# An RWKV block on eight cores: PSUM copies moved from VectorE to ScalarE, one product moved from VectorE to GpSimd

## The reference, cut to what matters

```python
xn = layer_norm(x, ln1_w, ln1_b);  lx = time_shift(xn)            # x: [8, 4096, 1024] f32
k = (xn*time_mix_k + lx*(1-time_mix_k)) @ w_key                   # v, r likewise
sr = sigmoid(r);  w = exp(time_decay)
# per channel, over t (numerically stabilised in the reference):
#   out_t = (A_t + e^(u+k_t) v_t) / (B_t + e^(u+k_t))
#   A_(t+1) = e^(-w) A_t + e^(k_t) v_t ;  B_(t+1) = e^(-w) B_t + e^(k_t)
x1 = x + (out*sr) @ w_output
xn2 = layer_norm(x1, ...);  fk, fr = projections of its time mixes
y = layer_norm(x + x1 + sigmoid(fr) * (square(relu(fk)) @ f_w_value))
out = layer_norm(y + (silu(y@Wg.T) * (y@Wu.T)) @ Wd.T)            # Wg, Wu, Wd from int32, scale 1/127
```

## Time and profile before

| | us |
|---|---|
| median of 3 timed runs | 5509.81 |
| lowest and highest of them | 5486.03, 5567.28 |
| the profiled execution | 5275.61 |
| its span, slowest core (core 3) | 5274.0 |
| shortest span of a core | 5226.8 |
| VectorE busy | 1458.3 (28%) |
| ScalarE busy | 881.8 (17%) |
| GpSimd busy | 145.7 (3%) |
| TensorE matmul busy | 2883.7 (55%) |

### The profile page before, as it was taken

One profiled execution on the slowest core, in us unless ns is written; L12 is line 12 of the kernel. 1 busy time (PEld: TensorE's weight loads), 2 busy tenths in 40 slices (PEclk: granted clock), 3 DMA queues, 4 the chain that ended last, 5 costly groups with the idle time before them and its releaser, 6 DMA issues.

```text
span 5274.0 us, 42491 instructions; the slowest of 8 cores (5226.8 to 5274.0 us)
## 1 busy us (share of the span) xinstructions
PE 2883.7 (55%) x14080; PEld 1449.4 (27%) x14080; DVE 1458.3 (28%) x2032; ACT 881.8 (17%) x1222; POOL 145.7 (3%) x328
## 2 busy tenths in 40 slices
PE   0444444520001777777773576765399999164554
PEld 0211121210000544444442232332144444021222
DVE  2233333236771444443441111111011111010101
ACT  1011111003221222223221112111011111001111
POOL 1100000000000000000000000000000000000000
PEclk9977767765555888888887787887699999587777
DMA  5333333443317222212215524332411010413132
GB/s 104 92 103 96 96 92 84 122 153 129 149 64 147 72 69 80 80 61 81 79 39 118 153 80 136 104 104 74 86 34 62 33 64 25 112 56 112 56 112 72
DMA packets 351012, 472.56 MB, mean 90 GB/s; under 512 B 83536, under 2 KB 263760, under 8 KB 345680
## 3 DMA queue, kind: packets, MB, share of 16 engines
q1 hardware_dynamic: 111488, 218.11, 12.7%
q10 hardware_dynamic: 215552, 186.67, 10.9%
q0 software_dynamic: 23760, 65.07, 6.9%
HBM read 293.65 MB, written 203.42 MB: 94 GB/s over the span
## 4 chain that ended last, share of the span: by engine, by line
issue 26%; PEld 19%; DMA 18%; DVE 12%; DVEq 8%; ACT 7%; ACTq 4%; PEldq 4%; another core or an unknown queue 2%; POOLq 1%; POOL 0%; SPq 0%
PEld psum L340 17%; DVEq L106 7%; DMA v_fm<-arena 4%; ACTq L106 4%; DMA k_fm<-arena 3%; PEldq L106 3%; DMA r_fm<-arena 3%; DMA arena<-h_fm 2%; DMA arena<-wd_bf 2%; ACT arena L297 2%; PEld psum L350 1%; POOLq L106 1%; DVE arena L498 1%; DVE arena L494 1%
## 5 line engine op out<-in xcount | busy, mean ns | idle before, releaser
L340 PE MATMUL psum<-arena 128*128 128x512 bf16 (+1 forms) x13312 | 2691.5, 364 | 1672.4 <-DMA arena<-wo 526.7
L340 PEld LDWEIGHTS psum<-arena 128*128 128x128 bf16 x13312 | 1334.3, 102 | 3024.9 <-issue 1998.8
L350 PE MATMUL psum<-arena 128*128 128x128 f32 x768 | 192.1, 380 | 689.0 <-ACTq L106 640.9
L297 ACT ACTIVATE arena<-arena 128x1024 f32<-128x1024 f32 x128 | 133.6, 1045 | 2327.8 <-DVEq L106 1496.0
L350 PEld LDWEIGHTS psum<-arena 128*128 128x128 f32 x768 | 115.1, 189 | 770.3 <-issue 770.3
L778 DVE SCALAR_TENSOR_TENSOR arena<-psum,arena 128x512 bf16<-128x512 f32 x192 | 123.7, 686 | 729.2 <-ACTq L106 729.2
L574 DVE TENSOR_SCALAR arena<-psum 128x256 f32<-128x256 f32 x512 | 181.6, 417 | 381.3 <-PEq L106 233.1
L392 DVE COPY arena<-psum 128x512 f32<-128x512 f32 x192 | 119.3, 684 | 434.3 <-DMA v_fm<-arena 163.2
L821 DVE SCALAR_TENSOR_TENSOR arena<-psum,arena 128x512 f32<-128x512 f32 x64 | 44.3, 692 | 672.5 <-PEq L106 663.1
L705 DVE SCALAR_TENSOR_TENSOR arena<-psum,arena 128x512 f32<-128x512 f32 x64 | 44.3, 692 | 670.9 <-PEq L106 664.9
L772 ACT ACTIVATE arena<-psum 128x512 bf16<-128x512 f32 x192 | 104.2, 594 | 610.6 <-PEq L106 604.2
(11 more groups left out here) (75 smaller groups left out, 879.6 us busy)
## 6 DMA issues: line engine op xcount, KB each, us to landing
fk_fm<-arena ACTq DMA_DIRECT2D x16, 2048.0 KB, 8.8
arena<-fk_fm SPq DMA_DIRECT2D x8, 4096.0 KB, 30.3
h_fm<-arena ACTq DMA_DIRECT2D x8, 3072.0 KB, 11.7
arena<-h_fm SPq DMA_DIRECT2D x8, 3072.0 KB, 16.9
arena<-x SPq DMA_DIRECT2D x8, 2048.0 KB, 9.2
k_fm<-arena ACTq DMA_DIRECT2D x64, 256.0 KB, 2.7
v_fm<-arena ACTq DMA_DIRECT2D x64, 256.0 KB, 2.7
r_fm<-arena ACTq DMA_DIRECT2D x64, 256.0 KB, 2.2
```

The costliest lines, as they stand in the source:

```text
L297: e.activation(dump.ap[:, q, :], xa[:, q, :], AF.Square, accum_out=stat.ap[:, 4 + q:5 + q])
L340: last = e.matmul(psumb.ap[:, 0:n], lts[i], rhs[i], start=(i == 0), stop=(i == cnt - 1))
L350: last = e.transpose(bank.ap[:, idx * 128:(idx + 1) * 128], ap, ident.ap)
```

## The change

Three things are done. (1) In stage 1 the four copies of `evac4` become ScalarE activations with the function Copy, in ScalarE's queue. (2) In stage 2 the product `ekv` goes to GpSimd as a tensor_tensor. `ek` gets two buffers and `rb` one instead of two. (3) In stage 2 the two scans are emitted as one operation, with one wait ahead and one drain behind them, and so are the first two combinations.

```diff
--- before.py
+++ after.py
@@ -389,9 +389,9 @@
 
                 def evac4(e, jobs=jobs, sgs=sgs):
                     for k4 in range(4):
-                        e.tensor_copy(sgs[k4].ap, jobs[k4][0].ap)
+                        e.activation(sgs[k4].ap, jobs[k4][0].ap, AF.Copy)
                     return e.nop()
-                B.op("vector", evac4, reads=[j[0] for j in jobs], writes=sgs)
+                B.op("scalar", evac4, reads=[j[0] for j in jobs], writes=sgs)
                 for k4, oc in enumerate(range(ob, ob + 4)):
                     B.op("scalar", lambda e, dst=dst, oc=oc, t0=t0, sg_=sgs[k4]: e.dma_start(
                         dst[oc * 128:(oc + 1) * 128, t0:t0 + 512], sg_.ap),
@@ -450,8 +450,8 @@
     ar.mark()
     kb2 = [ar.f32([128, 4096], f"kb{j}") for j in range(2)]
     vb2 = [ar.f32([128, 4096], f"vb{j}") for j in range(2)]
-    rb2 = [ar.f32([128, 4096], f"rb{j}") for j in range(2)]
-    ek = ar.f32([128, 4096], "ek")
+    rb = ar.f32([128, 4096], "rb")
+    ek2 = [ar.f32([128, 4096], f"ek{j}") for j in range(2)]
     ekv = ar.f32([128, 4096], "ekv")
     tmp = ar.f32([128, 4096], "tmp")
     Abuf = ar.f32([128, 4100], "Abuf")
@@ -465,7 +465,7 @@
 
     if debug_phases >= 2:
         for j in range(DC):
-            kb, vb, rb = kb2[j % 2], vb2[j % 2], rb2[j % 2]
+            kb, vb, ek = kb2[j % 2], vb2[j % 2], ek2[j % 2]
             yb, kmax = yb2[j % 2], kmax2[j % 2]
             for src, hb, b in ((k_fm, HB["k_fm"], kb), (v_fm, HB["v_fm"], vb),
                                (r_fm, HB["r_fm"], rb)):
@@ -475,7 +475,7 @@
             if j == 7 and "dbg" in debug_outs:
                 B.op("sync", lambda e: e.dma_start(dbg_h[:, 0:4096], rb.ap),
                      reads=[rb], dma=True)
-            B.op("scalar", lambda e, rb=rb: e.activation(
+            B.op("scalar", lambda e: e.activation(
                 tmp.ap, rb.ap, AF.Exp, scale=-1.0), reads=[rb], writes=[tmp])
             B.op("vector", lambda e, kmax=kmax, kb=kb: e.reduce_max(
                 kmax.ap[:, 0:1], kb.ap[:, 0:512], AX.X), reads=[kb], writes=[kmax])
@@ -485,28 +485,28 @@
             B.op("vector", lambda e, kmax=kmax: e.tensor_scalar(
                 kmax.ap[:, 1:2], kmax.ap[:, 1:2], 20.0, None, ALU.min),
                 reads=[kmax], writes=[kmax])
-            B.op("scalar", lambda e, kb=kb, kmax=kmax: e.activation(
+            B.op("scalar", lambda e, kb=kb, kmax=kmax, ek=ek: e.activation(
                 ek.ap, kb.ap, AF.Exp, bias=kmax.ap[:, 1:2]),
                 reads=[kb, kmax], writes=[ek])
-            B.op("vector", lambda e, vb=vb: e.scalar_tensor_tensor(
-                ekv.ap, ek.ap, 1.0, vb.ap, ALU.mult, ALU.mult),
+            B.op("gpsimd", lambda e, vb=vb, ek=ek: e.tensor_tensor(
+                ekv.ap, ek.ap, vb.ap, ALU.mult),
                 reads=[ek, vb], writes=[ekv])
-            B.op("vector", lambda e, j=j: e.tensor_tensor_scan(
-                Abuf.ap[:, 1:4097], dw.ap[:, j:j + 1].to_broadcast([128, 4096]),
-                ekv.ap, 0.0, ALU.mult, ALU.add),
-                reads=[ekv, dw], writes=[Abuf])
-            B.op("vector", lambda e, j=j: e.tensor_tensor_scan(
-                Bbuf.ap[:, 1:4097], dw.ap[:, j:j + 1].to_broadcast([128, 4096]),
-                ek.ap, 0.0, ALU.mult, ALU.add),
-                reads=[ek, dw], writes=[Bbuf])
-            B.op("vector", lambda e, j=j, kb=kb: e.scalar_tensor_tensor(
-                kb.ap, ekv.ap, eu.ap[:, j:j + 1], Abuf.ap[:, 0:4096],
-                ALU.mult, ALU.add),
-                reads=[ekv, eu, Abuf], writes=[kb])
-            B.op("vector", lambda e, j=j, vb=vb: e.scalar_tensor_tensor(
-                vb.ap, ek.ap, eu.ap[:, j:j + 1], Bbuf.ap[:, 0:4096],
-                ALU.mult, ALU.add),
-                reads=[ek, eu, Bbuf], writes=[vb])
+            def scans2(e, j=j, ek=ek):
+                e.tensor_tensor_scan(
+                    Abuf.ap[:, 1:4097], dw.ap[:, j:j + 1].to_broadcast([128, 4096]),
+                    ekv.ap, 0.0, ALU.mult, ALU.add)
+                return e.tensor_tensor_scan(
+                    Bbuf.ap[:, 1:4097], dw.ap[:, j:j + 1].to_broadcast([128, 4096]),
+                    ek.ap, 0.0, ALU.mult, ALU.add)
+            B.op("vector", scans2, reads=[ekv, ek, dw], writes=[Abuf, Bbuf])
+            def numden(e, j=j, kb=kb, vb=vb, ek=ek):
+                e.scalar_tensor_tensor(
+                    kb.ap, ekv.ap, eu.ap[:, j:j + 1], Abuf.ap[:, 0:4096],
+                    ALU.mult, ALU.add)
+                return e.scalar_tensor_tensor(
+                    vb.ap, ek.ap, eu.ap[:, j:j + 1], Bbuf.ap[:, 0:4096],
+                    ALU.mult, ALU.add)
+            B.op("vector", numden, reads=[ekv, ek, eu, Abuf, Bbuf], writes=[kb, vb])
             B.op("vector", lambda e, vb=vb: e.scalar_tensor_tensor(
                 ekv.ap, tmp.ap, 1.0, vb.ap, ALU.add, ALU.mult),
                 reads=[tmp, vb], writes=[ekv])
```

## The result

The changed kernel is 1.6% faster: the ratio of its time to that before is 0.984, with a 95% interval of 0.980 to 0.989. In some executions of either kernel the cores of a die run several per cent longer at a lower granted clock; the ratio leaves these out, but the plain medians over 26 runs each (5249.75 us against 5431.62) hold them, and the median of 5509.81 us that the prediction started from is of such runs alone. The profiled execution spans 5189.8 us on its slowest core, against 5274.0: 84 us less, where 40 were forecast.

The account below looks back on a forecast made before the run. No engine bounds the kernel; stage 1 is a cycle of about 123 us per block through ScalarE's queue, stage 2 strictly serial. Stage 1 -73 and stage 2 +33 gave -40 us: 5469 from 5509.81, range 5395 to 5530.

Parts of the forecast that it names:

- Stage 2, +33: Stage 2: product on GpSimd, handovers and merging together lose 4.2 us in each of eight tiles, +33 us.
- P: Stage 2: time of GpSimd's product, taken as 8.5 us with bounds 4.43 and 16.6.
- merging: Stage 2: emitting scans and combinations as one operation each, counted as saving 0.05 us.
- Second ek buffer and single r buffer, nothing: Stage 2: the second ek buffer buys nothing, since queue order and tmp hold L488; the single r buffer costs nothing.
- The first wait, -116: Stage 1: k0's copies no longer stand behind VectorE's mixes, gaining 7 x 16.6 = 116 us.
- k1, v1 and r1 "change nothing": Stage 1: these copies wait for staging buffers on either engine; four take 2.4 us on ScalarE, as on VectorE.
- It counts in full: 5.0 us a block.: Stage 1: v0's and r0's copies now fall between stores, 2.5 us each, 35 us for seven blocks.
- I give them the same mean time: Stage 1: stores meet the conversion DMAs as before, so their mean time stays the same.
- I would be wrong if the stores slowed down once they start earlier: Stage 1: a stated sign of failure, that stores slow down once they start earlier.
- 2.5 for k0 behind the loop: Stage 1: in block 7's projection, behind the loop, k0's copies also pay 2.5 us.
- The conversion chain as the next bound: Stage 1 rival: conversions ahead of L311 become the bound if lengthened over 7.5 us a block; 5500 us, chance 0.08.
- The starting point: Whole kernel: the forecast started from the timed median of 5509.81 us, 234 above the profiled execution, cause unknown.

Follow-up runs that it names:

- e6: The changed kernel with the product ekv back on VectorE, all else as changed; stage 2 took 473 us.
- e7: e3 with stage 2 pipelined: two buffers each for tmp and ek, next tile's exps emitted early, product on VectorE; ratio to before 0.958, stage 2 382 us.
- e1: The kernel before with only the copies moved to ScalarE; ratio to before 0.978, stage 1 998 us.
- e12: The kernel before plus four unused ScalarE copies ahead of v0's and r0's stores, making a pause between stores; stage 1 1125 us.
- e4: The kernel before with all 56 weight conversions emitted behind the last projection; blocks 1 to 6 of stage 1 were 108.3 us long.
- e5: e1 with all weight conversions emitted behind the last projection; blocks 1 to 6 of stage 1 were 96.1 us long.
- e3: e1 with the copies of v0 and r0 back on VectorE, the others staying on ScalarE; ratio to before 0.984, stage 1 982 us.
- e9: The changed kernel with the two scans separate again and the one over ek first; ratio to before 0.981, stage 2 508 us.
- e8: e7 with the next tile's product on GpSimd right behind the exps instead of on VectorE; stage 2 445 us.

## Why the prediction was wrong, point by point

- **Stage 2, +33.** Right in size (+32 as the cores' mean), with errors that nearly cancelled: P was 8.80 us where I took 8.5 (2.4 us over eight tiles), the handovers to and from GpSimd took a little more than I counted, and merging gave about 4 us where I counted 0.4. The Trainium skill's page "GPSIMD Engine Reference", section "Performance versus the Vector engine", led to an estimate of 9.0 us; the trace has 8.80, so it was a little closer than my slope from a 128-element row.
- **Second ek buffer and single r buffer, nothing.** Right: e6's tiles start as before. That `tmp` and queue order together were the tie is shown by e7, which undid both at once.
- **The first wait, -116.** Right in mechanism: VectorE's mixes no longer stand ahead. It measured 198.1 - 77.5 = 121 us.
- **k1, v1 and r1 "change nothing".** Mis-sized. Four copies take 2.07 us on ScalarE against 2.48, and these 24 copy groups stand on the chain: 24 x 0.41 = 10 of the 133.4 - 121.6 = 12 us. I had read 0.60 us as a mean and multiplied by four; the rows overlap.
- **"It counts in full: 5.0 us a block."** This is the step that failed. The gaps themselves, 16 of them, measured 42.2 - 6.6 = 36 us, where I had 35 + 5 = 40 (two of the three gaps behind the loop are among them). But the stores in fours fell by 15 us beside them (434 to 419; by 23 in e1), a term that I had set to zero with "I give them the same mean time". e12 has the same with the gap alone: 38 us of gaps, 26 us off the stores. e4 and e5 show that it needs the conversions. I had written that I would be wrong if the stores slowed down once they start earlier; they became faster.
- **Together**, on the cores' means: -121 + 36 - 12 - 15 + 3 = -109, against -116 + 40 + 2.5 = -73 in the same terms. The 3 us are everything outside the four columns, where I had 2.5 for k0 behind the loop. Of the 36 us between the two sums, 15 are the stores, 12 the copies, 5 the first wait and 4 the gaps. The stores are the largest, but the other three make more together, and all four errors lie on the same side.
- **The conversion chain as the next bound.** It came closer than I had thought. In block 5 the spare time of L311 fell from 19.14 us to 3.87; I had 7.5. (19.14 was not the least, as I wrote: in block 1 L311 waits for nothing but the conversions, in both kernels.) Over the eight cores and blocks 2 to 7 the mean spare time fell from 22.2 to 5.6 us, and in 3 of the 48 cases in the changed kernel there is none left (under 0.3 us); e1 has 8, e3 14 and e7 15. So the conversions now bound single blocks, and more of them the faster stage 1 is: e3 and e7 have blocks only 1 to 2 us shorter than e1 (105.2 and 105.5 against 106.7).

```profile
601.29 0.20 POOL L311 TENSOR_TENSOR arena<-arena 128x4 f32<-128x4 f32 x1 [3.87 <-ACTq L106]
```

- **The starting point.** The absolute forecast of 5469 us hung on a median 4% above the profiled execution. The text saw the 234 us and added them back without a cause; the range in us inherited them. As a difference it would have been 5234 for a span that came out at 5190.

What stays open: the 10 us of the rest, and why a store under the conversion traffic lands sooner behind a pause. The first stores of v0 and r0 alone account for 19 us in the changed kernel (67 to 48), more than the whole, and for 17 of the 26 in e12, but for only 8 of the 21 that e3 gave back. That a first store beside the last of the tensor before it is the costly one is therefore argued from the sums; no run here separates it from the pause.

## What to carry to other kernels

A copy that is off the critical engine can still be on the critical queue: what counted here was not the 119 us of VectorE work that went away, but that 25 us of mixes had stood ahead of the first copy in each block. A pause in a chain of DMAs that runs beside a second stream of DMAs can cost less than its length: here a third to a half with the conversions running, while without them (e4 and e5) the stores gave nothing back. And before a product moves to GpSimd to spare VectorE, look at what VectorE would do meanwhile: both kinds of instruction that were tried here beside the product, the scan and the combination, shared no time with it. No run tried one that reads a single tensor. And a second buffer belongs to the tile that ties the queues together, here `tmp`.

## What the runs showed of the hardware

- GpSimd multiplies two 128x4096 f32 tensors in 8.80 us, VectorE in 4.43.
- A VectorE scan excludes GpSimd's product as a combination of two tensors does, though one of its inputs is a single column read again and again: the product waited for all of its 8.69 us (17.12 us in all).
- In both orders seen, the one that started first ran to its end and the other waited, with a lead of 0.16 us (the scan in e9) and of 0.42 us (the product in e8).
- ScalarE's copies of 128x512 f32 from PSUM have a mean of 0.604 us and start every 0.49 us when issued together: four in 2.07 us, against VectorE's 2.48.
